# Skipping the out-of-range rows of a gather, with the destination filled beforehand

## The chip, the cores and the metric
The kernel runs on 1 core of one Trainium2 chip. The metric is the device time of one execution in microseconds: the median of the runs, unprofiled. TensorE is called PE here, VectorE DVE, ScalarE ACT, GpSimd POOL and SyncE SP.

## The reference
A recommendation model (DLRM): a small MLP over 13 dense features, 26 embedding lookups per sample, all pairwise dot products of the 26 embeddings, and one top layer over both.

```python
B = 2048; NUM_DENSE = 13; NUM_SPARSE = 26; VOCAB = 12500; EMB = 64
x = relu(dense_features @ W0 + b0)        # 13 -> 512
x = relu(x @ W1 + b1)                     # -> 256
dense_out = relu(x @ W2 + b2)             # -> 64
emb = vmap(lambda t, idx: t[idx], in_axes=(0, 1), out_axes=1)(tables, sparse_features)
gram = einsum('bid,bjd->bij', emb, emb)
interact = gram[:, TRIU_I, TRIU_J]        # 325 pairs, i < j
return concatenate([dense_out, interact], axis=1) @ Wt + bt    # -> 256
```

All is float32. `t[idx]` counts negative indices from the end and cuts indices past the end to the last row, 12,499. The index columns are drawn at random: columns 0, 2, 3, 18 and 24 from below 12,501, the other 21 from below about 99,990, all from small limits at or just above 0.

## The kernel before, in words
The 2048 samples are cut into 32 units of 64 samples; four units make a round, so there are 8 rounds. A unit's rows lie in `emb[:, j]`, one of four buffers (j is the unit's number in its round): partitions 0 to 63 hold the even index columns of the 64 samples, partitions 64 to 127 the odd ones, 13 columns (`NK`) of 64 floats each. So a unit takes 13 gathers (line 243), and each fetches 128 rows of 256 B, one per partition, at the row numbers that `row_idx[:, j, k]` holds. The 13 fall in three chunks of 8, 4 and 1, with a semaphore `rows_in[j][c]` each.

The row numbers are worked out once on DVE, in two parts (the first four units, then the rest): `wrap` and `capped` (lines 272, 273) apply the two rules for indices, `wrapped` (276) is their sum, and line 282 adds the start of the column's table (`field_base`, from POOL). The first part goes to `row_idx` straight, the others wait in `later_idx` and are copied to `row_idx` unit by unit (`stage_idx`, line 309), once the unit four before has been gathered.

POOL's program is nothing but the gathers after its start. Before the 13 gathers of a unit it waits that the transposes of the unit four before have read `emb[:, j]` (`rowsT_in_psum[LAST]`) and that its indices are staged (`idx_staged`).

For each unit PE transposes the rows chunk by chunk (line 481), DVE and ACT copy the transposed rows to `embT` (line 166, through `rowsT_evac`), PE computes the pairwise products of four samples at a time (`gram_products`, line 497, 32 matmuls in two halves), and DVE and ACT copy the blocks that are wanted to `gram` (line 180, through `gram_evac`). After two units PE runs the top layer for their 128 samples (`top`, lines 504 and 510) against `w_gram`, DVE copies the result (`out_evac`, line 324), and SP stores it (line 219). The MLP's layers (lines 442, 450, 457; activations 383, 390, 396) stand between the units of a round. Each engine has its order written out by hand (`tensor_round`, `vector_round`, `scalar_round`); semaphores with counts tie them.

SP's queue at the start: its half of the first indices (196), the rest of the indices (198), weights (200 to 203), then, once DVE has cleared `w_tri`, 25 loads of the rows of the triangle (208) and four transfers from `w_tri` to `w_gram` (214). After that it only stores results. The third unit of the first round is the last that does without `w_gram`: the first top product waits for it.

Of the kernel before, what the change touches and what calls it, by code (L numbers as in the profile page):

```python
# [5 lines left out]
def bass_dlrm_forward(  # L6
# [20 lines left out]
    P = 128  # L27
# [45 lines left out]
    with ctx:  # L73
# [11 lines left out]
        wrap = sb("wrap", [P, NU, NK])  # L85
        capped = sb("capped", [P, NU, NK])
        wrapped = sb("wrapped", [P, NU, NK])
        field_base = sb("field_base", [P, 1, NK], i32)

        later_idx = sb("later_idx", [P, NU, NK], u32)  # L90
        row_idx = sb("row_idx", [P, UR, NK], u32)
# [29 lines left out]
        base_ready = sem("base_ready")  # L121
        idx_in = [sem("idx_in_first"), sem("idx_in_rest")]
        idx_step = sem("idx_step")
        idx_ready = sem("idx_ready")
        later_ready = sem("later_ready")
        idx_staged = sem("idx_staged")
# [66 lines left out]
        @block.sync  # L193
        def _(sp):

            sp.dma_start(raw_idx[0:US, :, 0:UR // 2, :], sparse_v[:, :, 0:UR // 2, :]).then_inc(idx_in[0], 16)
            for x in range(2):
                sp.dma_start(raw_idx[x * US:(x + 1) * US, :, UR // 2:NP, :], sparse_v[:, :, UR // 2:NP, :]).then_inc(
                    idx_in[1], 16)
            sp.dma_start(w1_sb[:, :, :], w1.rearrange("(c p) n -> p c n", p=P)).then_inc(mlp_w_in, 16)  # L200
            sp.dma_start(w2_sb[:, :, :], w2.rearrange("(c p) n -> p c n", p=P)).then_inc(mlp_w_in, 16)
            sp.dma_start(wd_sb[0:H2, :], wt[0:H2, :]).then_inc(w_top_in, 16)
            sp.dma_start(wd_sb[H2:H2 + 1, :], bt.rearrange("(a n) -> a n", a=1)).then_inc(w_top_in, 16)

            sp.wait_ge(tri_zeroed, 1)
            for i in range(F - 1):
                n = F - 1 - i
                sp.dma_start(w_tri[i:i + 1, i:F - 1, :],
                             wt[tri_row(i):tri_row(i) + n, :].rearrange("(a j) n -> a j n", a=1)).then_inc(tri_in, 16)

            sp.wait_ge(tri_in, 16 * (F - 1))
            for g in range(SQ):
                t0 = first_slot(g)
                sp.dma_start(w_gram[FP * g:FP * (g + 1), t0:NS, :],
                             w_tri[:, col(t0, g) - 1:F - 1:SQ, :]).then_inc(w_top_in, 16)
            with sp.Fori(0, ROUNDS) as r:
                for q in range(2):
                    sp.wait_ge(out_ready[q], r + 1)
                    sp.dma_start(out_v[:, bass.ds(r * 2 + q, 1), :], out_sb[:, q:q + 1, :]).then_inc(stored[q], 16)
            for q in range(2):  # L220
                sp.wait_ge(stored[q], 16 * ROUNDS)

        @block.gpsimd
        def _(pool):

            for x in range(2):
                nc.gpsimd.iota(field_base[x * US:(x + 1) * US, 0, :], pattern=[[2 * VOCAB, NK]],
                               base=x * VOCAB, channel_multiplier=0).then_inc(base_ready, 1)

            pool.wait_ge(base_ready, 2)  # L230
            pool.wait_ge(zeros_set, 1)
            nc.gpsimd.affine_select(out=ident[:, :], in_=ident[:, :], pattern=[[-1, P]], base=0,
                                    channel_multiplier=1, compare_op=ALU.not_equal, fill=1.0).then_inc(ident_ready, 1)

            def gather(r, j):

                wait_if_any(pool, rowsT_in_psum[LAST], r * UR + j + 1 - UR)
                wait_if_any(pool, idx_staged, r * UR + j + 1 - UR)

                nc.gpsimd.nop(nofuse=True)  # L240
                for c, ks in enumerate(CHUNKS):
                    for k in ks:
                        nc.gpsimd.indirect_dma_start(  # L243
                            emb[:, j, k, :], None, tables_v[:, :],
                            bass.IndirectOffsetOnAxis(ap=row_idx[:, j, k:k + 1], axis=0),
                        ).then_inc(rows_in[j][c], 16)


            pool.wait_ge(idx_ready, 1)
            for j in range(UR):  # L250
                gather(0, j)
            with pool.Fori(1, ROUNDS) as r:
                for j in range(UR):
                    gather(r, j)

        @block.vector
        def _(dve):
            nc.vector.memset(ident[:, :], 0.0).then_inc(zeros_set, 1)
            steps = [0]


            for part, (u0, u1) in enumerate(PARTS):
                dve.wait_ge(idx_in[part], 32)
                halves = [(slice(x * US, (x + 1) * US),
                           raw_idx[x * US:(x + 1) * US, :, u0 // 2:u1 // 2, x:F:2].rearrange("s h t k -> s t h k"))
                          for x in range(2)]

                def by_unit(buf, rows):
                    return buf[rows, u0:u1, :].rearrange("s (t h) k -> s t h k", h=2)

                for rows, raw in halves:
                    nc.vector.tensor_scalar(by_unit(wrap, rows), raw, 0.0, float(VOCAB), ALU.is_lt, ALU.mult)
                    last = nc.vector.tensor_scalar(by_unit(capped, rows), raw, float(VOCAB - 1), None, ALU.min)
                last.then_inc(idx_step, 1)
                dve.wait_ge(idx_step, 2 * part + 1)
                nc.vector.tensor_tensor(wrapped[:, u0:u1, :], capped[:, u0:u1, :], wrap[:, u0:u1, :],
                                        ALU.add).then_inc(idx_step, 1)
                dve.wait_ge(idx_step, 2 * part + 2)
                if part == 0:
                    dve.wait_ge(base_ready, 2)  # L280
                dst = row_idx[:, :, :] if part == 0 else later_idx[:, 0:NU - UR, :]
                nc.vector.scalar_tensor_tensor(
                    out=dst, in0=wrapped[:, u0:u1, :], scalar=0.0,
                    in1=field_base[:, :, :].to_broadcast([P, u1 - u0, NK]), op0=ALU.max,
                    op1=ALU.add).then_inc(idx_ready if part == 0 else later_ready, 1)


            nc.vector.memset(embT[:, :, :, :], 0.0)
            nc.vector.memset(gram[:, :, 0, :], 0.0)
            nc.vector.memset(later_idx[:, NU - UR:NU, :], 0)  # L290
            nc.vector.memset(h2[H2:H2 + 1, :], 1.0).then_inc(consts_set, 1)
            nc.vector.memset(w_tri[:, :, :], 0.0)
            nc.vector.memset(w_gram[:, 0, :], 0.0).then_inc(tri_zeroed, 1)

            dve.wait_ge(consts_set, 1)
            dve.wait_ge(later_ready, 1)

            def embT_evac(r, j):

                n = r * UR + j  # L300

                wait_if_any(dve, gram_in_psum, (n - 1) * 2)
                for c in range(len(CHUNKS)):
                    dve.wait_ge(rowsT_in_psum[c], n + 1)
                    rowsT_evac(nc.vector.tensor_copy, c, 0, j).then_inc(embT_even[c], 1)

            def stage_idx(r, j):

                nc.vector.tensor_copy(row_idx[:, j:j + 1, :],  # L309
                                      later_idx[:, bass.ds(r * UR + j, 1), :]).then_inc(idx_staged, 1)  # L310

            def gram_blocks(r, j):

                if j % 2 == 0:
                    wait_if_any(dve, top_in_psum[j // 2], r)
                for half in range(2):
                    dve.wait_ge(gram_in_psum, (r * UR + j) * 2 + half + 1)
                    gram_evac(nc.vector.tensor_copy, DVE_BLOCKS, j, half).then_inc(gram_evac_dve, 1)

            def out_evac(r, q):  # L320
                dve.wait_ge(top_in_psum[q], r + 1)

                wait_if_any(dve, stored[q], r * 16)
                nc.vector.tensor_copy(out_sb[:, q, :], mlp_ps[q][:, 0:NO]).then_inc(out_ready[q], 1)  # L324

            def vector_round(r, first=False):
                for j in range(UR):
                    embT_evac(r, j)
                    stage_idx(r, j)

                    if j == 0 and not first:
                        out_evac(r - 1, 1)
                    if j == 3:
                        out_evac(r, 0)
                    gram_blocks(r, j)


            vector_round(0, first=True)
            with dve.Fori(1, ROUNDS) as r:
                vector_round(r)  # L340
            out_evac(ROUNDS - 1, 1)
# [230 lines left out]
```

## Time and profile before
| what | value |
|---|---|
| time, median of 2 runs (unprofiled) | 543.76 us (543.75 to 543.78) |
| span of the profiled execution, first to last instruction | 754.1 us |
| time of the profiled execution beyond its span | not given |
| mean granted TensorE clock | 0.694 of full speed |
| busy: PE, DVE, ACT, POOL | 353.1, 204.3, 201.5, 394.4 us |
| packets of the gathers' queue | 13312, 13.66 MB, 13.0% of 16 engines' span |
| read from HBM, written | 15.18 MB, 2.10 MB |

The profiled execution is far longer than the unprofiled ones of the same program. A row of a timeline gives the start and the length in us of an instruction, or of several in a row, then the engine (SPq and ACTq are the queues that issue DMAs), the line, the operation, what is written and what is read. An idle time in brackets is followed by what ended it: another instruction, a DMA, "issue" (nothing that the profile shows) or "remote" (something outside what it knows).

### The profile page before, as it was taken

The page shows a single profiled execution, that of the slowest core. Times are in us where ns is not written, and L with a number is a line of the kernel's source. Part 1 is how long each engine was busy: PE and PEld are TensorE (multiplying, and loading weights), DVE is VectorE, ACT ScalarE, POOL GpSimd, SP SyncE. Part 2 cuts the span into 40 slices and gives each one's busy share as a digit, 9 for nine tenths or more (in the row PEclk, how much of TensorE's full clock was granted, in tenths as well). Part 3 has the DMA queues.
Part 4 walks back from the last instruction along what each step waited for, and adds up shares of the span by engine and source line. Part 5 has one row for each costly group of instructions (what it writes and reads, how often), then busy time and mean ns, then how long its engine had stood idle before and what let it go on. Part 6 is the DMA issues. An engine that isn't in the chain of part 4 may idle for free.

```text
span 754.1 us, 6098 instructions
## 1 busy us (share of the span) xinstructions
PE 353.1 (47%) x1744; PEld 301.2 (40%) x1744; DVE 204.3 (27%) x675; ACT 201.5 (27%) x637; POOL 394.4 (52%) x423
## 2 busy tenths in 40 slices
PE   2400075433753535435654247543275353543797
PEld 1400064322643524435543236443264352443675
DVE  6200022323132132231322312232313313223334
ACT  1010033212242133321322313321224203332354
POOL 5777444554655544666445565455465554466000
PEclk9955568666775657756577677766667665775688
DMA  3231111111111111111111111111111111111000
GB/s 82 42 72 26 18 16 18 27 20 26 24 17 28 27 16 18 23 29 26 16 16 26 21 30 19 16 26 19 24 23 17 26 27 16 18 23 29 7 0 15
DMA packets 19047, 18.23 MB, mean 24 GB/s; under 512 B 8535, under 2 KB 12345, under 8 KB 19020
## 3 DMA queue, kind: packets, MB, share of 16 engines
q0 software_dynamic: 13312, 13.66, 13.0%
q1 hardware_dynamic: 4532, 4.31, 1.8%
q10 hardware_dynamic: 1194, 0.16, 0.2%
q8 instruction: 4, 0.07, 0.0%
q14 instruction: 5, 0.04, 0.0%
HBM read 15.18 MB, written 2.10 MB: 23 GB/s over the span
## 4 chain that ended last, share of the span: by engine, by line
another core or an unknown queue 46%; PE 21%; ACT 20%; issue 10%; DVE 2%; DMA 0%; ACTq 0%
ACT gram L180 12%; PE gram_ps L497 9%; ACT embT L166 6%; PE mlp_ps L510 4%; PE mlp_ps L442 3%; PE mlp_ps L457 2%; PE rowsT_ps L481 2%; DVE gram L180 1%; DVE embT L166 1%; ACT h L390 1%; ACT h L383 1%; PE mlp_ps L504 1%; PE mlp_ps L450 0%; DMA x_sb<-in_r_dense_features_dram 0%
## 5 line engine op out<-in xcount | busy, mean ns | idle before, releaser
L243 POOL DMA_INDIRECT emb<-in_L_rec_tables_dram,row_idx x416 | 393.6, 946 | 301.0 <-DVE row_idx L309 178.9
L180 ACT COPY gram<-gram_ps 32x48 f32<-32x48 f32 (+1 forms) x512 | 122.5, 239 | 394.4 <-remote 268.4
L180 DVE COPY gram<-gram_ps 32x48 f32<-32x48 f32 (+1 forms) x512 | 121.4, 237 | 380.3 <-remote 244.0
L481 PE MATMUL rowsT_ps<-ident,emb 128*128 128x128 f32 (+1 forms) x224 | 41.3, 295 | 386.2 <-ACT embT L166 336.0
L481 PEld LDWEIGHTS rowsT_ps<-ident,emb 128*128 128x128 f32 (+1 forms) x224 | 27.2, 144 | 397.4 <-issue 391.2
L497 PEld LDWEIGHTS gram_ps<-embT 128*128 128x128 f32 x1024 | 165.3, 257 | 19.0 <-issue 17.9
L497 PE MATMUL gram_ps<-embT 128*128 128x100 f32 x1024 | 169.2, 341 | 5.4 <-DVE embT L166 4.9
L166 DVE COPY embT<-rowsT_ps 64x512 f32<-64x512 f32 (+2 forms) x96 | 62.9, 691 | 114.0 <-remote 76.4
L166 ACT COPY embT<-rowsT_ps 64x512 f32<-64x512 f32 x64 | 51.5, 874 | 96.8 <-remote 75.9
L510 PE MATMUL mlp_ps<-w_gram,gram 128*128 128x256 f32 x224 | 69.8, 472 | 2.0 <-ACT gram L180 2.0
L510 PEld LDWEIGHTS mlp_ps<-w_gram,gram 128*128 128x128 f32 x224 | 55.2, 249 | 13.7 <-DVE gram L180 2.3
L442 PE MATMUL mlp_ps<-xT,w_sb 13*128 (+1 forms) x64 | 30.2, 649 | 0.0
L450 PE MATMUL mlp_ps<-h,w_sb 128*128 128x256 f32 x128 | 29.1, 380 | 0.0
L450 PEld LDWEIGHTS mlp_ps<-h,w_sb 128*128 128x128 f32 x128 | 23.7, 190 | 2.9
L442 PEld LDWEIGHTS mlp_ps<-xT,w_sb 13*128 13x128 f32 x64 | 19.9, 325 | 6.3 <-issue 1.8
L383 ACT ACTIVATE h<-mlp_ps,b_sb 128x256 f32<-128x256 f32 x32 | 13.4, 472 | 27.7 <-PE mlp_ps L442 26.0
L324 DVE COPY out_sb<-mlp_ps 128x256 f32<-128x256 f32 x16 | 6.8, 424 | 45.8 <-issue 29.1
L457 PE MATMUL mlp_ps<-h,w_sb 128*64 128x256 f32 x32 | 14.9, 616 | 0.0
L504 PE MATMUL mlp_ps<-wd_sb,h 65*128 65x256 f32 x32 | 12.8, 492 | 0.0
L396 ACT ACTIVATE h<-mlp_ps,b_sb 64x256 f32<-64x256 f32 x8 | 3.8, 470 | 18.6 <-PE mlp_ps L457 18.6
L457 PEld LDWEIGHTS mlp_ps<-h,w_sb 128*64 128x64 f32 x32 | 5.7, 208 | 4.6 <-issue 4.3
L390 ACT ACTIVATE h<-mlp_ps,b_sb 128x256 f32<-128x256 f32 x16 | 6.7, 470 | 1.9 <-PE mlp_ps L450 1.5
(24 smaller groups left out, 35.1 us busy)
## 6 DMA issues: line engine op xcount, KB each, us to landing
emb<-in_L_rec_tables_dram,row_idx POOLq DMA_INDIRECT x416
out_dram<-out_sb SPq DMA_DIRECT2D x16, 128.0 KB, 1.7
w_gram<-w_tri SPq DMA_DIRECT2D x3, 192.0 KB
w_sb<-in_L_rec_W_dram SPq DMA_DIRECT2D x1, 512.0 KB
raw_idx<-n_r_sparse_features_dram SPq DMA_DIRECT2D x2, 182.0 KB
w_gram<-w_tri SPq DMA_DIRECT2D x1, 224.0 KB
x_sb<-in_r_dense_features_dram ACTq DMA_DIRECT2D x1, 104.0 KB, 3.0
w_sb<-in_L_rec_W_dram SPq DMA_DIRECT2D x1, 64.0 KB
```

The source lines that it names most:

```text
L166: return copy(dst[:, ks.start + odd:ks.stop:2], rowsT_ps[BANK[c]][odd * EMB:(odd + 1) * EMB, i:i + m])
L180: last = copy(gram[FP * g:FP * (g + 1), q, t0:NS, c0 + a0 * SQ + s:c0 + a1 * SQ:SQ], gram_ps[FP * s:FP * (s + 1), a0:a1, src:src + SQ * (N ...
L243: nc.gpsimd.indirect_dma_start(emb[:, j, k, :], None, tables_v[:, :], bass.IndirectOffsetOnAxis(ap=row_idx[:, j, k:k + 1], axis=0),).then_ ...
L383: last = nc.scalar.activation(h0[:, c, :], mlp_ps[half][:, m * RS:(m + 1) * RS], ACT.Relu, bias=b0_sb[:, c:c + 1])
L390: last = nc.scalar.activation(h1[:, m, :], mlp_ps[0][:, m * RS:(m + 1) * RS], ACT.Relu, bias=b1_sb[:, m:m + 1])
L442: last = nc.tensor.matmul(mlp_ps[half][:, m * RS:(m + 1) * RS], w0_sb[:, c * P:(c + 1) * P], xT[:, bass.ds(r * 2, 2), :], start=True, stop ...
L450: last = nc.tensor.matmul(mlp_ps[0][:, m * RS:(m + 1) * RS], w1_sb[:, c, m * P:(m + 1) * P], h0[:, c, :], start=(c == 0), stop=(c == H0 // ...
L457: last = nc.tensor.matmul(mlp_ps[1][0:H2, 0:RS], w2_sb[:, c, :], h1[:, c, :], start=(c == 0), stop=(c == H1 // P - 1))
L481: last = nc.tensor.transpose(rowsT_ps[BANK[c]][0:m * EMB, (k - 8 * BANK[c]) // 2, :, :], emb[:, j, k:k + m, :], ident[:, :])
L497: last = nc.tensor.matmul(gram_ps[:, a, 0:SQ * (F - 1)], samples.rearrange("p s f -> p (s f)"), samples[:, :, 1:F], start=True, stop=True)
L504: nc.tensor.matmul(mlp_ps[q][:, 0:NO], h2[:, q * P:(q + 1) * P], wd_sb[:, :], start=True, stop=False)
L510: last = nc.tensor.matmul(mlp_ps[q][:, 0:NO], gram[:, q, t, :], w_gram[:, t, :], start=False, stop=(t == NS - 1))
```

## The change
Row numbers of indices at or past the last row are made too large on purpose: `far` is 26 x 12,500 where the index is at or past 12,499 and 0 elsewhere, plus `field_base`. It takes the place of `field_base` in the last step. Every gather gets a bound, the last row of all tables, with the instruction not to treat a row number beyond it as an error; such rows are not fetched. So that the last row of the right table stands in their place, `last_rows` is loaded once (the last row of each of the 26 tables, repeated over 64 partitions), and SP copies it, 128 partitions x 3328 B, to `emb[:, j]` ahead of each unit's gathers. POOL waits for this copy (`filled[j]`) in place of the transposes; SP waits for the transposes in its stead. SP's stores are woven between the fills.

```diff
         wrapped = sb("wrapped", [P, NU, NK])
+        far = sb("far", [P, NU, NK])
         field_base = sb("field_base", [P, 1, NK], i32)
+        last_rows = sb("last_rows", [P, NK, EMB])
...
             sp.dma_start(raw_idx[0:US, :, 0:UR // 2, :], sparse_v[:, :, 0:UR // 2, :]).then_inc(idx_in[0], 16)
             for x in range(2):
+                sp.dma_start(last_rows[x * US:(x + 1) * US, :, :],
+                             tables[x:F:2, VOCAB - 1:VOCAB, :].rearrange("k v e -> v k e").to_broadcast([US, NK, EMB])
+                             ).then_inc(last_in, 16)
+            sp.wait_ge(last_in, 32)
+            for j in range(UR):
+                sp.dma_start(emb[:, j, :, :], last_rows[:, :, :]).then_inc(filled[j], 16)
+            for x in range(2):
                 sp.dma_start(raw_idx[x * US:(x + 1) * US, :, UR // 2:NP, :], sparse_v[:, :, UR // 2:NP, :]).then_inc(
                     idx_in[1], 16)
...
-            with sp.Fori(0, ROUNDS) as r:
-                for q in range(2):
-                    sp.wait_ge(out_ready[q], r + 1)
-                    sp.dma_start(out_v[:, bass.ds(r * 2 + q, 1), :], out_sb[:, q:q + 1, :]).then_inc(stored[q], 16)
+            def fill(r, j):
+                sp.wait_ge(rowsT_in_psum[LAST], (r - 1) * UR + j + 1)
+                sp.dma_start(emb[:, j, :, :], last_rows[:, :, :]).then_inc(filled[j], 16)
+
+            def store(r, q):
+                sp.wait_ge(out_ready[q], r + 1)
+                sp.dma_start(out_v[:, bass.ds(r * 2 + q, 1), :], out_sb[:, q:q + 1, :]).then_inc(stored[q], 16)
+
+            for j in range(UR):
+                fill(1, j)
+            store(0, 0)
+            with sp.Fori(1, ROUNDS - 1) as r:
+                fill(r + 1, 0)
+                store(r - 1, 1)
+                for j in range(1, UR):
+                    fill(r + 1, j)
+                store(r, 0)
+            store(ROUNDS - 2, 1)
+            store(ROUNDS - 1, 0)
+            store(ROUNDS - 1, 1)
...
             def gather(r, j):
 
-                wait_if_any(pool, rowsT_in_psum[LAST], r * UR + j + 1 - UR)
+                pool.wait_ge(filled[j], (r + 1) * 16)
                 wait_if_any(pool, idx_staged, r * UR + j + 1 - UR)
...
                             bass.IndirectOffsetOnAxis(ap=row_idx[:, j, k:k + 1], axis=0),
+                            bounds_check=F * VOCAB - 1, oob_is_err=False,
                         ).then_inc(rows_in[j][c], 16)
...
                 for rows, raw in halves:
                     nc.vector.tensor_scalar(by_unit(wrap, rows), raw, 0.0, float(VOCAB), ALU.is_lt, ALU.mult)
+                    nc.vector.tensor_scalar(by_unit(far, rows), raw, float(VOCAB - 1), float(F * VOCAB), ALU.is_ge, ALU.mult)
                     last = nc.vector.tensor_scalar(by_unit(capped, rows), raw, float(VOCAB - 1), None, ALU.min)
                 last.then_inc(idx_step, 1)
-                dve.wait_ge(idx_step, 2 * part + 1)
+                dve.wait_ge(idx_step, 3 * part + 1)
+                if part == 0:
+                    dve.wait_ge(base_ready, 2)
+                nc.vector.tensor_tensor(far[:, u0:u1, :], far[:, u0:u1, :],
+                                        field_base[:, :, :].to_broadcast([P, u1 - u0, NK]),
+                                        ALU.add).then_inc(idx_step, 1)
                 nc.vector.tensor_tensor(wrapped[:, u0:u1, :], capped[:, u0:u1, :], wrap[:, u0:u1, :],
                                         ALU.add).then_inc(idx_step, 1)
-                dve.wait_ge(idx_step, 2 * part + 2)
...
                     out=dst, in0=wrapped[:, u0:u1, :], scalar=0.0,
-                    in1=field_base[:, :, :].to_broadcast([P, u1 - u0, NK]), op0=ALU.max,
+                    in1=far[:, u0:u1, :], op0=ALU.max,
```

## Rows read from the trace of the kernel before

**Rows 1.** The page's first part: span, and busy time by engine with share and instruction count.
```profile
span 754.1 us, 6098 instructions
...
PE 353.1 (47%) x1744; PEld 301.2 (40%) x1744; DVE 204.3 (27%) x675; ACT 201.5 (27%) x637; POOL 394.4 (52%) x423
```

**Rows 2.** Busy time by stretch: before, during and after the gathers (start:end, length, engines).
```profile
5.48:696.30 690.82, 308.32 (x1515) 263.40 (x1513) 179.71 (x586) 176.65 (x559) 393.62 (x416) 0.68 0.16 25
696.30:754.10 57.80, 43.97 (x226) 37.16 (x226) 23.42 (x83) 23.84 (x79) 0.00 (x0) 0.80 0.02 8
```

**Rows 3.** The waits, POOL's three: engine, line, releaser: us in total, times, longest.
```profile
POOL emb L243 <- DVE row_idx L309: 178.9, 27, 14.6
POOL emb L243 <- issue: 118.3, 388, 0.3
...
POOL emb L243 <- DVE row_idx L282: 3.8, 1, 3.8
```

**Rows 4.** Instructions on the tile emb: ns least/median/most, first and last start.
```profile
L243 POOL DMA_INDIRECT emb<-in_L_rec_tables_dram,row_idx x416: 942/947/1105, 5.5 to 695.3; - x139
```

**Rows 5.** The timeline of POOL, then of PE: start us, us, instruction [idle before, releaser].
```profile
5.48 1.10 POOL L243 DMA_INDIRECT emb<-in_L_rec_tables_dram,row_idx  x1 [3.83 <-DVE row_idx L282]
6.89 0.95 POOL L243 DMA_INDIRECT emb<-in_L_rec_tables_dram,row_idx  x1 [0.30 <-issue]
...
14.39 0.95 POOL L243 DMA_INDIRECT emb<-in_L_rec_tables_dram,row_idx  x1 [0.30 <-issue]
...
17.55 1.09 PE L481 MATMUL rowsT_ps<-ident,emb 128*128 128x128 f32 x4 [9.24 <-DMA emb<-in_L_rec_tables_dram,row_idx]
```

**Rows 6.** The timeline of unit 28's transposes and copies; then line 180's idle time by releaser.
```profile
686.10 0.82 PE L481 MATMUL rowsT_ps<-ident,emb 128*128 128x128 f32 x6
...
695.30 1.13 ACT L166 COPY embT<-rowsT_ps 64x512 f32<-64x512 f32 x1 [3.74 <-issue]
695.30 1.13 DVE L166 COPY embT<-rowsT_ps 64x512 f32<-64x512 f32 x1 [3.75 <-issue]
...
  remote: 512.4, 64
```

**Rows 7.** The timeline behind the last gather.
```profile
706.27 3.71 PE L497 MATMUL gram_ps<-embT 128*128 128x100 f32 x32
...
708.23 4.05 ACT L180 COPY gram<-gram_ps 32x48 f32<-32x48 f32 x16 [8.78 <-PE gram_ps L497]
...
718.02 6.17 PE L497 MATMUL gram_ps<-embT 128*128 128x100 f32 x32
...
721.79 2.01 ACT L180 COPY gram<-gram_ps 32x48 f32<-32x48 f32 x8 [2.82 <-PE gram_ps L497]
...
739.25 0.27 PE L481 MATMUL rowsT_ps<-ident,emb 128*64 128x128 f32 x1
...
740.16 3.79 PE L497 MATMUL gram_ps<-embT 128*128 128x100 f32 x32 [0.64 <-DVE embT L166]
742.19 4.03 ACT L180 COPY gram<-gram_ps 32x48 f32<-32x48 f32 x16 [3.08 <-PE gram_ps L497]
...
746.36 4.95 PE L510 MATMUL mlp_ps<-w_gram,gram 128*128 128x256 f32 x14 [1.96 <-ACT gram L180]
751.35 0.42 DVE L324 COPY out_sb<-mlp_ps 128x256 f32<-128x256 f32 x1 [5.13 <-PE mlp_ps L510]
```

**Rows 8.** The timeline of the start: index loads, index work on DVE, weight loads of SP.
```profile
1.58 1.47 SPq L198 DMA_DIRECT2D raw_idx<-n_r_sparse_features_dram  x2
...
3.09 0.60 SPq L200 DMA_DIRECT2D w_sb<-in_L_rec_W_dram  x1
...
3.50 0.18 DVE L272 TENSOR_SCALAR wrap<-raw_idx 64x52 f32<-64x52 int32 x1 [2.48 <-DMA raw_idx<-n_r_sparse_features_dram]
3.60 0.17 DVE L273 TENSOR_SCALAR capped<-raw_idx 64x52 f32<-64x52 int32 x1
...
4.11 0.21 DVE L276 TENSOR_TENSOR wrapped<-capped,wrap 128x52 f32<-128x52 f32 x1
...
6.14 0.58 DVE L272 TENSOR_SCALAR wrap<-raw_idx 64x364 f32<-64x364 int32 x1 [1.58 <-DMA raw_idx<-n_r_sparse_features_dram]
...
20.80 28.74 SPq L208 DMA_DIRECT2D w_tri<-in_L_rec_Wt_dram  x25
...
50.43 6.61 SPq L214 DMA_DIRECT2D w_gram<-w_tri  x4
```

**Rows 9.** DMA issues: out<-in, engine, count, KB each, us from issue to landing.
```profile
out_dram<-out_sb SPq DMA_DIRECT2D x16, 128.0 KB, 1.7
...
x_sb<-in_r_dense_features_dram ACTq DMA_DIRECT2D x1, 104.0 KB, 3.0
```

More of the change, by code:

```diff
@@ L123, in bass_dlrm_forward @@
         idx_step = sem("idx_step")
+        last_in = sem("last_in")
+        filled = [sem(f"filled_{j}") for j in range(UR)]
         idx_ready = sem("idx_ready")
@@ L272, in _ @@
                     nc.vector.tensor_scalar(by_unit(wrap, rows), raw, 0.0, float(VOCAB), ALU.is_lt, ALU.mult)
+                    nc.vector.tensor_scalar(by_unit(far, rows), raw, float(VOCAB - 1), float(F * VOCAB), ALU.is_ge, ALU.mult)
                     last = nc.vector.tensor_scalar(by_unit(capped, rows), raw, float(VOCAB - 1), None, ALU.min)
                 last.then_inc(idx_step, 1)
-                dve.wait_ge(idx_step, 2 * part + 1)
+                dve.wait_ge(idx_step, 3 * part + 1)
[4 more added lines that the diff above has]
+                                        ALU.add).then_inc(idx_step, 1)
                 nc.vector.tensor_tensor(wrapped[:, u0:u1, :], capped[:, u0:u1, :], wrap[:, u0:u1, :],
                                         ALU.add).then_inc(idx_step, 1)
-                dve.wait_ge(idx_step, 2 * part + 2)
-                if part == 0:
-                    dve.wait_ge(base_ready, 2)
+                dve.wait_ge(idx_step, 3 * part + 3)
                 dst = row_idx[:, :, :] if part == 0 else later_idx[:, 0:NU - UR, :]
```

## The prediction, made before the change was run

> **What bounds the kernel now.** I began with the spans and the page's engine rows: the profiled execution spans 754.1 us, and no engine is busy for more than 52% of it; POOL, with 394.4 us, is the busiest [rows 1]. The median of the unprofiled runs is 543.76 us, so the profiled execution is 210 us longer than the thing to be predicted, and its shares can't be carried over before that is explained. (The profile gives no time of this execution beyond its span; I make the sum against the span and then set it beside the median.)
>
> Next I read POOL's own waits, because they split its time without remainder. The first gather starts at 5.48 us and the last ends at 696.3; the stretch between holds 416 gathers, 393.6 us busy, and no other POOL work [rows 2]. Its idle time is 388 gaps of the "issue" kind, 118.3 us, so 0.305 us each, and 27 waits for DVE's copy of the next indices (line 309), 178.9 us [rows 3]. 5.48 + 393.6 + 118.3 + 178.9 = 696.3, and the tail behind it is 57.8 us, which makes the 754.1.
>
> Then the gathers one by one: 942 to 947 ns each, only the first is 1105 [rows 4], started every 1.25 us without a break when nothing holds them [rows 5]. The length doesn't depend on k, though the fields differ much in how many distinct rows they hit. DMA engines are 16% busy in that stretch [rows 2], so POOL's own making of the gathers, not the moving of rows, is what takes time.
>
> Are the 178.9 us of waits real? In the traced execution PE's transposes of one unit start at 686.10 and take 0.82 us, yet both copies that wait for them start at 695.30, marked as waiting for nothing that the profile shows; the same happens 64 times before line 180 (512.4 us over both engines, "remote") [rows 6]. As soon as POOL is silent, behind 696.3, such a delay is gone: the copies follow the grams within 2 us [rows 7]. If the untraced kernel has no such delays, POOL never waits, and its time is 5.48 + 416 x 0.946 + 415 x 0.305 = 525.6 us to the end of the last gather, then the landing (the eighth gather ends at 15.34 and the transposes that it releases start at 17.55: 2.2 us [rows 4, 5]), then the last unit from its last transpose at 739.25 to the end at 754.1, 14.9 us [rows 7]. Sum 542.7, against a median of 543.76. That fits within 0.2%, and it is my reading: untraced, the kernel is **a chain of 416 back-to-back POOL gathers with 23 us around it**. Written for later: T = 23.3 + 416 p, with p the period of a gather (1.251 now) and 1.1 us unexplained left in the 23.3.
>
> **How much is skipped.** 21 of the 26 index columns are drawn up to about 99,990 and are cut to the last row from 12,499 on: 87.5% of their values. The other five (0, 2, 3, 18, 24) stay below 12,501. Of 26 x 128 half-rows 5 + 21 x 0.125 = 7.6 columns' worth stay: 29%; 71% of the rows aren't gathered any more. The number of gather instructions stays 416.
>
> **Part by part.**
> Start. SP issues the two broadcasts of the last rows, waits for them, then issues four fills, and the first gather now waits for the first fill. The nearest rows: two index loads of such a broken-up kind take SP from 1.58 to 3.05, and DVE has their data at 6.14, 3.1 us later [rows 8]. Then issue and landing of a fill of 416 KB: issue 0.6 us as for w1, landing not shown; bounds are 1.7 us (a store of 128 KB) and 5 us, and I take 2.8, near the 3.0 of the 104 KB load [rows 8, 9]. 6.1 + 0.6 + 2.8 = 9.5 instead of 5.48: **+4.0 us** (bounds +3 and +7). The Trainium skill (DMA: Bandwidth & Descriptors, "Anatomy of one DMA") would price the fill at 2.0 us plus bytes over 436 GB/s, an estimate of 3.0 us; no row here shows it.
> Index work on DVE. Two more tensor_scalar and one tensor_tensor for the first part, 0.18 + 0.18 + 0.21 us [rows 8]: the indices are there at about 5.2 instead of 4.6, still ahead of the fill at 9.5, so nothing. Without that cover it would be 0.6 us.
> What SP issues later. The rest of the indices now goes behind four fills, some 8 us later; with it DVE's memsets, w_tri (20.8 then about 29) and w_gram (issued by 57.0, then 65) move [rows 8]. DVE is ready for unit 0 at about 28.7, and that unit's rows are there at 9.5 + 16.3 + 2.2 = 28.0. w_gram is wanted by the top product behind unit 3's transposes, at about 9.5 + 4 x 16.3 + 2 = 77: nothing, and at most 2 us if the gathers get very short.
> Fills in the loop. 32 fills, one per unit; each waits until unit n-4 has been transposed, and the gather waits for it instead of for that transpose. Unit n-4's rows landed three units earlier, 3 x 16.3 = 49 us before POOL wants the buffer; the fill wants some 4 us and the chain ahead of it some 5 to 12. Hidden, with more than 30 us to spare. On SP, the fills of units 1 to 3 stand behind the store of the round before; its out_ready comes with the top product right behind unit 0's transposes, a unit earlier than the next fill is wanted. Nothing either. If that cover fails, a fill costs 4 us, 28 times, 112 us.
> DMA. The engines carry 416 KB more per unit and some 290 KB less of gathered rows; at 16% busy [rows 2] that is free.
> The gather itself is the term that decides. No row shows a gather with a bound. p consists of the 0.305 us gap, which I keep, and 0.946 us on POOL. Bounds of the gain: nothing (the dropped rows are still walked, or are written as empty entries), and 0.946 x 0.71 = 0.67 us (all of the busy time goes by rows). A loss isn't excluded, see below. Neither end has a near row, so I split the busy time in three equal parts, the fixed handling, reading and turning each index into an address, and writing its entry for the DMA engines; only the last goes with a dropped row. That gives 0.946 / 3 x 0.71 = **0.223 us** less, p = 1.028. It is a choice between the ends, not a measurement.
> Sum: 23.3 + 4.0 + 416 x 1.028 = **455 us**.
>
> A rule of the skill cuts both ways here. The trace shows that POOL's length is the same for all 416 gathers [rows 4]. The Trainium skill (DMA: Bandwidth & Descriptors, "SWDGE vs HWDGE vs iDMA") says that the GpSimd core computes one descriptor pair per piece before anything moves; by it a dropped row drops its share whole, and the time would go to the floor below. The same page ("Why a DMA increments its semaphore by 16 and not by 1") says that on this path all 16 engines post their count whatever the shape; that part would stay with every gather, and speaks for a small gain.
>
> **Rivals.**
> Floor: the gathers get so short that compute binds. In the tail, where nothing is late, a round goes from the grams of unit 28 at 706.27 to the end of the next top product at 751.3, at a granted clock of 0.80: 45.0 us [rows 2, 7]. First grams at about 31, then 8 x 45 and 2.8 for the last store: **394 us**. It decides from p = 0.88 on, that is once a gather's busy time falls by 0.37 us. For it: a gather's time can hardly be anything but work per row, since it waits for no data. Against: half of it may be fixed. Chance 0.2; the same mechanism with a smaller gain, 410 to 532 us, is my forecast, 0.3.
> No gain: dropped rows are walked and written as cheaply or as dearly as kept ones. T = 23.3 + 4.0 + 520.4 = **548 us**, +0.7%. For it: the length of 942 to 947 ns has no spread at all, as of work that runs over 128 entries whatever they hold. Chance 0.24. That the change doesn't do what it says (nothing is found beyond the bound) gives this time too.
> The bound makes the gather dearer: comparing each index, and closing gaps in a list of entries that was regular. Its place is the 0.946 us. It decides from 0.016 us per gather on (that puts 27.3 + 416 p over 554.6), 0.13 ns a row, where a row costs 7.4 ns now; a tenth of 0.946 more gives 587 us, a fifth 626, twice the time 941. For it: 7.4 ns a row is tight, and a compare with a branch is easily a tenth of it. Against: 71% of the rows have nothing behind the compare. Chance 0.26, most of it below 600.
> The fill as a new wait in the loop would show as POOL waiting for SP's DMA, at most +112 us; 30 us of slack speak against it, and I give it no share of its own.
>
> **How the numbers follow.** Gain of any size 0.5, no change 0.24, dearer 0.26. About 2% (11 us) either way is what a measurement of this kernel can't be told from no change by. Point 455. The range reaches from just under the floor, 392, over the no-gain case to 590: it leaves out about 0.12 above and 0.05 below. Cases of both signs hold much of the chance; the forecast's own range is 410 to 532.
>
> **What the profile after would show.** The gather's busy mean on POOL decides: near 0.72 right, 0.946 the no-gain case, above it the dear one. A spread by k would show cost by rows (k = 1 keeps all 128, k = 0, 9 and 12 keep 72, the others 16). The first gather should start near 9.5 us. In the traced execution POOL's waits should be named for the fills instead of line 309, and since its waits for compute are inflated there already, its span may grow even if the kernel gets faster. I am wrong if the untraced time isn't 27 + 416 p, or if POOL waits for fills with no inflated delay ahead of them.

## The result: 4.9% slower

The changed kernel takes 569.83 us (568.77 and 570.89 in two runs), the kernel before 543.76: a ratio of 1.049, 95% interval 1.043 to 1.055. The forecast was 455 us in a range of 392 to 590, with half of the chance on a gain. The time lies in the range, at the dear end, and on the other side of no change.

Beside the experiments the kernel before ran 21 more times, 20 of them took 542.1 to 544.9 us and one 735.7, and whether the trace ahead of the prediction, with its span of 754.1 us, is of that rare kind stays open, since its granted clock was 0.69 and that run's 1.00. The kernel before was profiled again (e0, below), and that trace, with a span of 542.0 us and a time of 543.8, is what the one after is compared with.

The page of the changed kernel, its first part and its DMA queues (queue, kind: packets, MB, share of 16 engines' span), then two groups of DMA issues (KB each, median us to landing):

```profile
span 567.0 us, 6574 instructions
...
PE 357.3 (63%) x1744; PEld 291.8 (51%) x1744; DVE 211.1 (37%) x681; ACT 204.8 (36%) x637; POOL 415.4 (73%) x423
...
q1 hardware_dynamic: 10836, 18.37, 9.2%
q0 software_dynamic: 13312, 4.17, 4.8%
...
emb<-last_rows SPq DMA_DIRECT2D x32, 416.0 KB, 3.0
...
last_rows<-in_L_rec_tables_dram SPq DMA_DIRECT2D x2, 208.0 KB, 4.5
```

q0 is the gathers' queue. It moves 4.17 MB instead of 13.66, and the number of its packets is 13312 as before, 32 for each of the 416 gathers. q1 carries the fills.

The size of each packet in the trace says what becomes of a dropped row. Half of the packets, 16 for each gather, are of 4 bytes before and after. The other 16 stand for eight rows each. Before, all of them have 2048 bytes, 8 x 256. In the changed kernel they have 2048, 1796, 1292, 1040, 788, 536, 284 or 32 bytes: 256 for each row that is fetched, and 4 for each of the eight that is dropped. Counted so, 15,596 of the 53,248 rows are fetched, 29%, as worked out from the draws. So the rows are dropped, but a dropped row isn't taken out of the list: it leaves 4 bytes. What these carry no run shows.

The gathers themselves, and the two groups of fills behind them (ns least/median/most, first and last start):

```profile
L270 POOL DMA_INDIRECT emb<-in_L_rec_tables_dram,row_idx x416: 992/997/1140, 10.8 to 550.9; - x139
...
L229 SPq DMA_DIRECT2D emb<-last_rows x28: 464/465/1622, 49.7 to 488.7; - x28
L207 SPq DMA_DIRECT2D emb<-last_rows x4: 541/608/966, 7.1 to 9.0; - x4
```

This answers to [rows 4], and it is most of what the change does to the time: **997 ns instead of 944** (e0; 947 in [rows 4]), and as level as before. Sorted by k over the whole timeline, the middle gather is 1.00 us long for every k, for k = 1, which keeps all 128 rows, and for those that keep 16. What POOL waited for:

```profile
POOL emb L270 <- issue: 124.9, 410, 0.3
POOL emb L270 <- DMA emb<-last_rows: 9.2, 1, 9.2
POOL emb L270 <- DVE row_idx L341: 1.5, 5, 0.3
```

One wait for a fill, the first; none in the loop. The gaps between gathers are 124.9 us / 410 = 0.305, unchanged. Where that first wait comes from stands in the timeline of the start (start us, us, engine and line):

```profile
1.59 1.52 SPq L202 DMA_DIRECT2D last_rows<-in_L_rec_tables_dram  x2
...
4.77 0.21 DVE L314 SCALAR_TENSOR_TENSOR row_idx<-wrapped,far 128x52 uint32<-128x52 f32 x1
...
7.12 2.85 SPq L207 DMA_DIRECT2D emb<-last_rows  x4
...
10.85 1.14 POOL L270 DMA_INDIRECT emb<-in_L_rec_tables_dram,row_idx  x1 [9.20 <-DMA emb<-last_rows]
```

The last rows are issued until 3.1 and take 4.5 us to land, the first fill is issued at 7.12, and the first gather starts at 10.85, though its row numbers were there at 4.98. Last, the first and last gather and the end on PE, of the kernel before (e0) and then of the changed one:

```profile
5.37 1.10 POOL L243 DMA_INDIRECT emb<-in_L_rec_tables_dram,row_idx  x1 [3.73 <-DVE row_idx L282]
...
523.61 0.94 POOL L243 DMA_INDIRECT emb<-in_L_rec_tables_dram,row_idx  x1 [0.30 <-issue]
...
527.14 0.27 PE L481 MATMUL rowsT_ps<-ident,emb 128*64 128x128 f32 x1
...
534.25 4.95 PE L510 MATMUL mlp_ps<-w_gram,gram 128*128 128x256 f32 x14 [1.95 <-DVE gram L180]
```

```profile
550.89 0.99 POOL L270 DMA_INDIRECT emb<-in_L_rec_tables_dram,row_idx  x1 [0.30 <-issue]
...
553.92 0.27 PE L513 MATMUL rowsT_ps<-ident,emb 128*64 128x128 f32 x1
...
561.05 3.26 PE L542 MATMUL mlp_ps<-w_gram,gram 128*128 128x256 f32 x14 [1.96 <-DVE gram L184]
```

And the stretch of the last fourteen top products of each (start:end, length, busy time by engine, granted clock, DMA share, GB/s):

```profile
534.25:539.20 4.95, 4.94 (x14) 3.69 (x14) 0.00 (x0) 0.00 (x0) 0.00 (x0) 0.66 0.01 3
```

```profile
561.05:564.30 3.25, 3.25 (x14) 2.54 (x14) 0.00 (x0) 0.00 (x0) 0.00 (x0) 1.00 0.02 5
```

From these rows the difference adds up. The first gather starts 10.85 - 5.37 = 5.5 us later. From the first gather's start to the last one's it is 518.24 us before and 540.04 after: +21.8, which is 415 times 0.0525. From the last gather's start to the end of the span it is 18.4 before and 16.1 after: -2.3, of which 1.7 is that the last fourteen top products ran 3.26 us, at a granted clock of 1.00 (2.4 GHz), instead of 4.95, at 0.66 in the mean; the matmuls are the same. This -2.3 can't be put down to the change: in e1 the same stretch takes 20.3 us, in e2, with all that the change adds, 18.3. Sum +25.0 us, and the spans are 542.0 and 567.0.

### The profile page after: what moved, and what is told of

The parts are those of the page before. It is cut to its first block, busy times and chain, and to the rows that moved or that the text cites. A ratio compares the mean times of both kernels' runs of the same rounds, so it can differ in the third digit from the quotient of the medians.

```text
span 567.0 us, 6574 instructions
## 1 busy us (share of the span) xinstructions
PE 357.3 (63%) x1744; PEld 291.8 (51%) x1744; DVE 211.1 (37%) x681; ACT 204.8 (36%) x637; POOL 415.4 (73%) x423
## 3 DMA queue, kind: packets, MB, share of 16 engines
q0 software_dynamic: 13312, 4.17, 4.8%
## 4 chain that ended last, share of the span: by engine, by line
POOL 70%; issue 23%; POOLq 3%; DMA 2%; PE 1%; DVE 1%; SPq 0%; DVEq 0%
POOL emb L270 70%; POOLq L270 2%; PE mlp_ps L542 1%; DMA last_rows<-in_L_rec_tables_dram 1%; DVE gram L184 1%; DMA emb<-last_rows 0%; DMA emb<-in_L_rec_tables_dram,row_idx 0%; PE gram_ps L529 0%; POOLq L73 0%; SPq L202 0%; POOLq L193 0%; SPq L200 0%; POOLq L267 0%; POOLq L280 0%; PE rowsT_ps L513 0%
## 5 line engine op out<-in xcount | busy, mean ns | idle before, releaser
L270 POOL DMA_INDIRECT emb<-in_L_rec_tables_dram,row_idx x416 | 414.6, 997 | 135.6 <-issue 124.9
L513 PE MATMUL rowsT_ps<-ident,emb 128*128 128x128 f32 (+1 forms) x224 | 57.4, 363 | 195.1 <-DMA emb<-in_L_rec_tables_dram,row_idx 160.0
L529 PEld LDWEIGHTS gram_ps<-embT 128*128 128x128 f32 x1024 | 142.0, 225 | 18.2 <-issue 16.1
L529 PE MATMUL gram_ps<-embT 128*128 128x100 f32 x1024 | 145.9, 309 | 5.4 <-DVE embT L170 5.4
L513 PEld LDWEIGHTS rowsT_ps<-ident,emb 128*128 128x128 f32 (+1 forms) x224 | 30.9, 171 | 219.6 <-DMA emb<-in_L_rec_tables_dram,row_idx 136.7
L542 PE MATMUL mlp_ps<-w_gram,gram 128*128 128x256 f32 x224 | 81.1, 531 | 2.0 <-DVE gram L184 2.0
L542 PEld LDWEIGHTS mlp_ps<-w_gram,gram 128*128 128x128 f32 x224 | 63.0, 285 | 16.7 <-DVE gram L184 2.3
L536 PE MATMUL mlp_ps<-wd_sb,h 65*128 65x256 f32 x32 | 16.1, 603 | 0.0
L489 PE MATMUL mlp_ps<-h,w_sb 128*64 128x256 f32 x32 | 9.5, 424 | 0.0
L536 PEld LDWEIGHTS mlp_ps<-wd_sb,h 65*128 65x128 f32 x32 | 8.1, 311 | 0.0
```

Source lines behind the costliest of these rows:

```text
L270: nc.gpsimd.indirect_dma_start(emb[:, j, k, :], None, tables_v[:, :], bass.IndirectOffsetOnAxis(ap=row_idx[:, j, k:k + 1], axis=0), bounds ...
L489: last = nc.tensor.matmul(mlp_ps[1][0:H2, 0:RS], w2_sb[:, c, :], h1[:, c, :], start=(c == 0), stop=(c == H1 // P - 1))
L513: last = nc.tensor.transpose(rowsT_ps[BANK[c]][0:m * EMB, (k - 8 * BANK[c]) // 2, :, :], emb[:, j, k:k + m, :], ident[:, :])
L529: last = nc.tensor.matmul(gram_ps[:, a, 0:SQ * (F - 1)], samples.rearrange("p s f -> p (s f)"), samples[:, :, 1:F], start=True, stop=True)
L536: nc.tensor.matmul(mlp_ps[q][:, 0:NO], h2[:, q * P:(q + 1) * P], wd_sb[:, :], start=True, stop=False)
L542: last = nc.tensor.matmul(mlp_ps[q][:, 0:NO], gram[:, q, t, :], w_gram[:, t, :], start=False, stop=(t == NS - 1))
```

## The experiments

Theory A: giving a gather a bound costs POOL some 0.05 us, whatever the bound drops. Rivals: the fills disturb POOL (B); dropping rows is what costs (C). And a question behind them: why did dropping 71% of the rows save nothing?

**e0, the kernel before once more.** No edit.

> The kernel before, unchanged, profiled once more. If the 210 us between its traced span and its untraced time come from the tracing, the next trace may show another span; if the span stays 754 us with a time of 543.8, the tracing adds it steadily. Without the delays I expect a span near 542 us, with POOL's start at 5.5, gathers of 0.946 us, 0.305 us apart, without waits, and a tail of 17 us.

Measured: 543.8 us, span 542.0. POOL's waits in this trace:

```profile
POOL emb L243 <- issue: 124.6, 409, 0.3
POOL emb L243 <- DVE row_idx L282: 3.7, 1, 3.7
POOL emb L243 <- PE rowsT_ps L481: 1.8, 6, 0.3
```

```profile
L243 POOL DMA_INDIRECT emb<-in_L_rec_tables_dram,row_idx x416: 940/944/1098, 5.4 to 523.6; - x139
```

The 178.9 us of waits of [rows 3] are gone, and so is every "remote" wait of [rows 6]. The reading that the kernel is a chain of back-to-back gathers holds (sum 542.7, span 542.0). The reason that I gave for the long trace, the tracing, isn't borne out: this execution was traced too. What made the other one long stays open.

**e1, the bound alone.** The kernel before with one line more.

```diff
                             bass.IndirectOffsetOnAxis(ap=row_idx[:, j, k:k + 1], axis=0),
+                            bounds_check=F * VOCAB - 1, oob_is_err=False,
```

> The kernel before with a bound on every gather and nothing else; every row number lies inside it. Theory A (the bound itself costs the 0.051 us that a gather takes longer after the change): the gather's busy mean is 0.997 us, the time 543.8 + 416 x 0.051 = 565.0 us. Theory B (the fills disturb POOL) and theory C (dropping rows is what costs): 0.946 us, 543.8 us.

Measured: 567.23 us, ratio 1.044 (1.037 to 1.050). The page's first line, and the gathers:

```profile
span 565.7 us, 6514 instructions
...
L243 POOL DMA_INDIRECT emb<-in_L_rec_tables_dram,row_idx x416: 992/997/1140, 5.5 to 545.4; - x139
```

Nothing is dropped and nothing is filled, and a gather takes 997 ns, as in the changed kernel. This is theory A. The bound also adds one instruction per gather, 6514 instead of 6098: a register move of 29 ns in POOL's program. POOL's gaps are 124.6 us / 409 = 0.305 as before, so the move doesn't lengthen them, and the 53 ns stand in the gather itself.

**e2, fills and bound, nothing dropped.**

```diff
-                    nc.vector.tensor_scalar(by_unit(far, rows), raw, float(VOCAB - 1), float(F * VOCAB), ALU.is_ge, ALU.mult)
+                    nc.vector.tensor_scalar(by_unit(far, rows), raw, float(VOCAB - 1), 0.0, ALU.is_ge, ALU.mult)
```

> The changed kernel with far set to the table's start alone, so that no row number passes the bound: fills and bound stay, every row is fetched. Theory A: gather 0.997 us, time 569.8 us, as the changed kernel. Theory B: the same, 569.8. Theory C: gather 0.946, time 569.8 - 21.2 = 548.6 us.

Measured: 571.32 us, ratio 1.052 (1.049 to 1.055).

```profile
L270 POOL DMA_INDIRECT emb<-in_L_rec_tables_dram,row_idx x416: 992/997/1241, 10.9 to 551.1; - x139
```

**e3, everything dropped.**

```diff
-                    nc.vector.tensor_scalar(by_unit(far, rows), raw, float(VOCAB - 1), float(F * VOCAB), ALU.is_ge, ALU.mult)
+                    nc.vector.tensor_scalar(by_unit(far, rows), raw, -2.0e9, float(F * VOCAB), ALU.is_ge, ALU.mult)
```

> The changed kernel with every row number put past the bound, so that no row is fetched (the outputs are those of the last rows alone). Theories A and B: gather 0.997 us whatever is dropped, time 569.8 us. Theory C: the extra grows with the dropped share, 0.051 / 0.71 = 0.072 us, gather 1.018, time 578.6 us. My forecast's idea that a dropped row saves its entry: below 0.997.

Measured: 572.73 us, ratio 1.053 (1.050 to 1.057).

```profile
L270 POOL DMA_INDIRECT emb<-in_L_rec_tables_dram,row_idx x416: 992/997/1244, 10.5 to 551.4; - x139
```

```profile
q0 software_dynamic: 13312, 0.24, 1.7%
```

Between e2 (no row dropped), the changed kernel (71%) and e3 (all) the gather doesn't move by a nanosecond in the median. With all rows dropped, 0.24 MB are left and still 13312 packets: for each gather 16 of 4 bytes and 16 of 32, which is 4 bytes for each of the eight dropped rows. Theory C falls, and with it the idea of my forecast that a dropped row saves its entry's time.

**e5, no fills in the loop.** Only the first four fills stay; the gather waits for the transposes again.

```diff
             def fill(r, j):
-                sp.wait_ge(rowsT_in_psum[LAST], (r - 1) * UR + j + 1)
-                sp.dma_start(emb[:, j, :, :], last_rows[:, :, :]).then_inc(filled[j], 16)
+                pass
...
-                pool.wait_ge(filled[j], (r + 1) * 16)
+                pool.wait_ge(filled[j], 16)
+                wait_if_any(pool, rowsT_in_psum[LAST], r * UR + j + 1 - UR)
```

> The changed kernel with only the first four fills; later units keep whatever rows the buffer held where they skip (so the output differs). Bound and skipping stay. Theory A: gather 0.997 us, time 569.8 us. Theory B (the fills disturb POOL): gather 0.946, 569.8 - 21.2 = 548.6 us. Theory C: 569.8 us.

Measured: 571.34 us, ratio 1.050 (1.048 to 1.052), against 569.83 for the changed kernel in other runs.

```profile
L270 POOL DMA_INDIRECT emb<-in_L_rec_tables_dram,row_idx x416: 992/997/1284, 10.8 to 551.9; - x139
```

The 28 fills in the loop, 416 KB each, cost nothing that is measurable. Theory B falls, by e1 too, which has no fill at all.

**e7, the start undone.** The first four units are gathered whole, the last rows are loaded behind the other weights.

```diff
-                pool.wait_ge(filled[j], (r + 1) * 16)
+                wait_if_any(pool, filled[j], r * 16)
...
-                    in1=far[:, u0:u1, :], op0=ALU.max,
+                    in1=far[:, u0:u1, :] if part else field_base[:, :, :].to_broadcast([P, u1 - u0, NK]), op0=ALU.max,
```

> The changed kernel with the first four units gathered whole, without fills; the last rows are loaded behind the other weights, and the fills begin with the second round. POOL's first gather starts at 5.5 instead of 10.85 us, everything else stays. If the start costs what the trace says, the time is 569.8 - 5.3 = 564.5 us, and all the rest is the gather; if the start was hidden, 569.8 us.

Measured: 566.26 us, ratio 1.042 (1.039 to 1.044). 

```profile
L268 POOL DMA_INDIRECT emb<-in_L_rec_tables_dram,row_idx x416: 992/997/1256, 5.8 to 546.9; - x139
```

POOL starts at 5.8 us, and the time is 3.6 us below the changed kernel's, 5.1 below e5's, which ran beside it. It is also that of e1 (567.23), the bound alone. So bound and start together are all of the 4.9%.

**e4 and e10, fewer rows per gather.** The other partitions' rows are loaded once at the start.

```diff
-                            emb[:, j, k, :], None, tables_v[:, :],
-                            bass.IndirectOffsetOnAxis(ap=row_idx[:, j, k:k + 1], axis=0),
+                            emb[0:US, j, k, :], None, tables_v[:, :],
+                            bass.IndirectOffsetOnAxis(ap=row_idx[0:US, j, k:k + 1], axis=0),
```

> The kernel before with gathers of 64 partitions instead of 128: the odd columns' rows are not fetched, their half of the buffers is loaded once at the start with other rows (so the output differs), which moves POOL's start to about 10 us. Measures how much of a gather's 0.946 us goes by rows named in the instruction. If all of it does: 0.47 us, and the time falls to the floor near 400 us. If a third of it is fixed: 0.63, period 0.94, time 23.3 + 4.5 + 389 = 417 us. If it is fixed: 0.946 us and 548 us.

Measured: 534.02 us, ratio 0.982 (0.979 to 0.984), with a first gather that starts 6.4 us later than e0's.

```profile
L244 POOL DMA_INDIRECT emb<-in_L_rec_tables_dram,row_idx x416: 899/903/1014, 11.8 to 513.1; - x139
```

e10 names 16 partitions instead of 64 in the same two places.

> Gathers of 16 partitions instead of 128 (the rest of the buffers is loaded once, so the output differs). From 0.946 us at 128 rows and 0.903 at 64 a straight line gives 0.903 - 48 x 0.00067 = 0.871 us at 16 rows, and a time of 534.0 - 416 x 0.032 = 520.7 us. If the cost goes in steps instead (groups of rows handled together), 0.903 or well below 0.871.

Measured: 510.07 us, ratio 0.937 (0.933 to 0.941).

```profile
L244 POOL DMA_INDIRECT emb<-in_L_rec_tables_dram,row_idx x416: 842/847/977, 12.3 to 490.3; - x139
```

Halving the rows takes 0.041 us off a gather (944 to 903), going down to 16 another 0.056: 0.6 and 1.2 ns per row, no straight line. An eighth of the rows still costs 847 ns. So nearly nine tenths of the 944 ns don't go by the rows that a gather names, and even if a dropped row had cost nothing, a gather with 37 of 128 rows left would have come to somewhere between 847 and 903 ns, and the bound's own cost on top. The trace notes 128 active channels for a gather of 64 and of 16 rows too, so these runs don't tell a fixed handling of the instruction from a walk over all 128 partitions.

**e8, the bound on half the rows.** e4's kernel with e1's line.

> The kernel of half-size gathers (64 partitions, the other half of the buffers loaded once, so the output differs), with the bound added. Without it a gather took 0.903 us. Theory A1 (the bound costs a fixed 0.051 us per instruction): 0.954 us, time 534.0 + 21.3 = 555.3 us. Theory A2 (it costs 0.4 ns for each row that is compared): 0.903 + 0.026 = 0.929 us, time 544.7 us.

Measured: 551.30 us, ratio 1.014 (1.011 to 1.017).

```profile
L244 POOL DMA_INDIRECT emb<-in_L_rec_tables_dram,row_idx x416: 938/942/1062, 12.5 to 529.8; - x139
```

The bound adds 39 ns at 64 rows (942 against 903) and 53 at 128 (997 against 944), so neither of the two theories. A straight line through these two points would be some 25 ns for each instruction and 0.2 ns for each row; two traces of the kernel before differ by 3 ns (944 and 947), so this split is rough. At 128 rows the cost is the same whether rows are dropped or not.

**e9, the bound without skipping.**

```diff
+                            bounds_check=F * VOCAB - 1, oob_is_err=True,
```

> The kernel before with the bound, but a row number past it counts as an error instead of being skipped (none is past it). If comparing costs the time: gather 0.997 us and 565 us, as with the bound in skip mode. If only the skip mode costs: 0.946 us and 543.8 us.

Measured: 572.81 us, ratio 1.052 (1.049 to 1.055).

```profile
L243 POOL DMA_INDIRECT emb<-in_L_rec_tables_dram,row_idx x416: 1006/1011/1158, 5.7 to 551.6; - x139
```

It is the bound that costs, not the skipping; asking for an error instead of a skip costs 14 ns more, with no row past the bound in e9 or e1.

**e6, the floor.** Only the gathers of even k; the other columns keep rows loaded at the start.

```diff
-                    for k in ks:
+                    for k in ks[::2]:
...
-                    pe.wait_ge(rows_in[j][c], (r + 1) * (16 * len(ks)))
+                    pe.wait_ge(rows_in[j][c], (r + 1) * (16 * len(ks[::2])))
```

> The kernel before with the gathers of the odd k left out (7 of 13 per unit; the other columns keep rows loaded once at the start, so the output differs). POOL then needs 7 x 1.251 = 8.8 us per unit, less than the 11.3 us that compute took per unit in the tail of the first trace. My floor: 394 us, some 3 us more by the later start. If compute had hidden waits beside the gathers, it would be clearly above 400.

Measured: 401.22 us (399.54 and 402.90), ratio 0.738 (0.733 to 0.741). The chain that ended last, by line:

```profile
by line: PE gram_ps L501 28.4%; PE mlp_ps L514 14.6%; DVE gram L181 11.1%; PE mlp_ps L454 7.0%; PE mlp_ps L446 6.5%; issue 6.2%; DVE embT L167 5.8%; ACT embT L167 4.2%; PE rowsT_ps L485 3.7%; ACT gram L181 2.1%; PE mlp_ps L508 2.1%; PE mlp_
```

POOL has left the head of the chain: a gram product leads it. Two runs, so 401 is a figure to within 2 us; the floor worked out from the tail, 394 and 3 for the later start, was near. It was worked out from a stretch at a granted clock of 0.80, and e6 ran at 0.87, so part of the nearness is luck.

## Why the prediction went wrong, step by step

**What bounds the kernel: right.** A chain of 416 back-to-back gathers, sum 542.7 against a span of 542.0. Its formula carries over: 27.3 + 416 x 1.301 (540.04 / 415 in the changed kernel's trace, 0.997 of it busy) is 568.5, against 569.83 measured. That it comes so near is in part luck, since the start is 1.5 us dearer than its term and the end of this trace 2.3 us shorter than e0's. The 1.1 us left over are now accounted for: the sum lies 0.7 us above e0's span, and e0's time 1.8 us above it. Only the cause given for the long trace isn't borne out.

**The gather's price: wrong, and this decided it.** The step was "I split the busy time in three equal parts [...] only the last goes with a dropped row. That gives [...] 0.223 us less". The sum put the bound itself at nothing. Measured: 0.053 us more, all of it the bound's (e1). The split failed twice. First, the size: between 128 and 16 rows the part that goes by rows isn't a third of 0.946 us but a tenth, 97 ns (e4, e10). Second, the kind: none of it goes when a row is dropped (e2, the changed kernel and e3 are all at 997 ns), and the packets show that "writing its entry" didn't fall away: a dropped row still leaves 4 bytes. The split into thirds had no row behind it, and no row of the kernel before could have given one. Its gathers all name 128 rows, so their level length fits a fixed cost and a sum over 128 equal rows alike; it takes gathers that name fewer rows (e4, e10) to tell the two apart. For the same reason "a row costs 7.4 ns now", on which the floor and the dear case lean, was a mean and not a price: a row that isn't named saves 0.6 to 1.2 ns.

**The no-gain case: right about the dropped rows.** It said "dropped rows are walked and written as cheaply or as dearly as kept ones", with a chance of 0.24, and that is what e2, the changed kernel and e3 show. The forecast treated it and the dear case as rivals; they hold together, and 548 us plus 416 x 0.053 is 570.

The two rules of the skill came out as follows. The Trainium skill (DMA: Bandwidth & Descriptors, "SWDGE vs HWDGE vs iDMA") has one descriptor pair computed per DMA op. What I drew from it, that a dropped row drops its share whole, isn't what the trace shows: 4 bytes are left of each, and the length stays. The same page ("Why a DMA increments its semaphore by 16 and not by 1") has all 16 engines count whatever the shape. The 16 packets of 4 bytes for each gather, at 128, 64 and 16 rows and with 0, 71 and 100% of the rows dropped, agree with it.

**The dear case: right in sign, its size half of the one named.** "It decides from 0.016 us per gather on" and "a tenth of 0.946 more gives 587": it is 0.053 us, a twentieth. It had 0.26. Of its two reasons, "closing gaps" falls, since the length is the same with 0, 71 and 100% of the rows dropped. "Comparing each index" fits the part that grows from 64 to 128 rows, 14 of the 53 ns; what POOL does in the rest no run shows.

**The start: right in kind, +5.5 instead of +4.0 us**, inside the bounds of +3 to +7. The last rows landed in 4.5 us rather than 3.1, so the first fill was issued at 7.12 and not 6.1; the 32 fills' landing had a median of 3.0 us, near the 2.8 taken. The estimate of 3.0 us by the Trainium skill (DMA: Bandwidth & Descriptors, "Anatomy of one DMA") agrees, but the page gives its fit for DMAs that GpSimd issues, and these are issued by SP, so the agreement is one of these fills. e7 bears out that it isn't hidden.

**Index work, later loads, fills in the loop, DMA traffic: rightly costed at nothing.** POOL's waits name one fill, the first; e5 shows no gain from leaving the others out.

**The floor: near in size (397 expected for e6, 401 measured, at a higher clock), never reached by dropping rows.**

## What to carry to other kernels

If an engine is bound by issuing instructions, measure how their length moves with the work named in them before pricing a cut of that work: one run with fewer rows per gather (e4) and one with the bound alone (e1) would have priced both terms. A level length over instructions that all name the same amount of work tells nothing of it. Here most of the length doesn't move: an eighth of the rows still took 510 us, little more than half of the instructions took 401. And any option added to each of them is paid in full: 0.053 us times 416 is 22 us. Dropping bytes from a queue that is 16% busy saves bytes, not time. Where a trace's span lies far above the measured times, take apart which of its waits these times can hold before building on them, as the sum here did.

## What the runs showed of the hardware that was not expected

- A gather of 128 rows of 256 B takes POOL 944 ns, of 64 rows 903, of 16 rows 847, each with 0.30 us to the next.
- A bound adds 53 ns to it at 128 rows, the same with 0, 71 and 100% of the rows beyond it, and 39 ns at 64 (none beyond it); as an error instead of a skip it adds 67 ns at 128 rows.
- A row that is dropped by the bound still leaves 4 bytes in the gathers' queue, in the place of its 256, and the number of packets per gather stays 32: 16 of rows and 16 of 4 bytes.
